# Last self-attention: V stationary in the weighing, a fixed place behind q's and k's halves, the division on POOL, and VectorE's output addition ahead of statistics, scaling and quantising

## The reference, cut to what matters

```python
def _L1_attn_ref(x, W_qkv, W_out):
    ...
    q = rotary_embedding(q, seq_len, HEAD_DIM)
    k = rotary_embedding(k, seq_len, HEAD_DIM)
    scale = 1.0 / jnp.sqrt(jnp.asarray(HEAD_DIM, dtype=x.dtype))
    scores = jnp.einsum('bqhd,bkhd->bhqk', q, k) * scale
    mask = jnp.tril(jnp.ones((seq_len, seq_len), dtype=bool))[None, None, :, :]
    scores = jnp.where(mask, scores, NEG_INF)
    weights = jax.nn.softmax(scores, axis=-1)
    out = jnp.einsum('bhqk,bkhd->bqhd', weights, v)
    out = out.reshape(batch, seq_len, NUM_HEADS * HEAD_DIM)
    return jnp.einsum('bsf,fe->bse', out, W_out)
...
x = x + _L1_attn_ref(_layernorm(x, axis=-1), L1_attn_W_qkv, L1_attn_W_out)
x = x + _L1_ffn_ref(_layernorm(x, axis=-1), L1_ffn_weight)
```

## Time and profile before

| | before |
|---|---|
| median of 3 runs | 2555.43 us (2554.0 to 2556.09) |
| the profiled execution: its time | 2553.02 us |
| its span, first to last instruction | 2551.1 us |
| busy: PE, DVE, ACT, POOL | 93%, 71%, 49%, 33% of the span |
| mean granted TensorE clock | 0.969 |

### The profile page before, as it was taken

The page is one execution under the profiler, slowest core; times in us unless marked ns, Lnnn a source line. Parts: engine busy times, 40 slices in busy tenths (PEclk is TensorE's granted clock), DMA queues, the critical chain, the costliest instruction groups (busy, mean ns, idle before and its releaser), DMA issues. The chain is left out here.

```text
span 2551.1 us, 103353 instructions
## 1 busy us (share of the span) xinstructions
PE 2381.0 (93%) x44640; PEld 1961.5 (77%) x44640; DVE 1817.8 (71%) x3828; ACT 1251.6 (49%) x2826; POOL 840.3 (33%) x741
## 2 busy tenths in 40 slices
PE   7999999999989939999996999999997999999997
PEld 6888888888855537888875777777776888888885
DVE  6778777778867872222226888888896788888886
ACT  5666666665545532333225777776763323233232
POOL 3233333333321213344335444444222232323231
PEclk9999999999989959999998999999998999999998
DMA  6455555554414271111116887887772000000000
GB/s 202 139 155 156 153 156 157 157 151 131 112 31 136 79 305 53 50 49 47 51 54 203 240 231 224 227 233 223 214 205 74 3 3 3 11 11 11 11 11 26
DMA packets 199682, 298.98 MB, mean 117 GB/s; under 512 B 29496, under 2 KB 107452, under 8 KB 197952
## 3 DMA queue, kind: packets, MB, share of 16 engines
q1 hardware_dynamic: 192416, 275.58, 36.6%
q0 software_dynamic: 6816, 16.79, 2.0%
HBM read 170.75 MB, written 78.77 MB: 98 GB/s over the span
## 5 line engine op out<-in xcount | busy, mean ns | idle before, releaser
L846 ACT ACTIVATE prob_x<-ps_score_x,neg_max_x 128x257 f32<-128x257 f32 x1024 | 402.6, 479 | 204.8 <-DVE neg_max_x L914 204.8
L914 DVE TENSOR_REDUCE neg_max_x<-ps_score_x 128x2 f32<-128x514 f32 x512 | 328.9, 684 | 103.4 <-PE ps_score_x L730 102.2
L741 PEld LDWEIGHTS ps_v_x<-v_wide_x,probT_x 128*32 128x32 f32 x18432 | 289.3, 109 | 125.4 <-issue 118.4
L741 PE MATMUL ps_v_x<-v_wide_x,probT_x 128*32 128x68 f32 x18432 | 337.0, 224 | 24.8 <-issue 17.9
L938 DVE STREAM_TRANSPOSE probT_x<-prob_x 128x1152 f32<-128x1152 f32 x256 | 344.1, 1344 | 0.1
L1080 POOL TENSOR_TENSOR ctxT_x_lo<-ready,ctxT_x_hi 128x514 fp32r<-128x514 f32 x128 | 153.0, 1195 | 368.7 <-ACT ctxT_x_hi L825 311.8
L2444 POOL TENSOR_TENSOR rot_s<-turned_s,swapped_s 128x512 f32<-128x512 f32 x128 | 164.3, 1295 | 326.9 <-DVE swapped_s L2373 283.9
L1080 POOL TENSOR_TENSOR split<-loaded,split 128x514 fp32r<-128x514 f32 x128 | 153.5, 1200 | 329.4 <-ACT split L825 314.8
L231 PE MATMUL ps_x<-split,w_q_x_hi 128*128 128x258 f32 x1024 | 208.8, 301 | 13.3 <-POOL split L1080 10.1
L1984 DVE TENSOR_TENSOR hid_moe<-ps_up_moe,silu_moe 128x512 f32<-128x512 f32 x71 | 49.1, 692 | 203.5 <-PE ps_up_moe L231 203.5
L730 PE MATMUL ps_score_x<-kT_x,q_x 32*64 32x257 f32 x4096 | 177.6, 402 | 12.6 <-ACT prob_x L846 9.1
(11 more groups left out here) (299 smaller groups left out, 5967.5 us busy)
## 6 DMA issues: line engine op xcount, KB each, us to landing
v_wide_x<-v_x SPq DMA_DIRECT2D x512, 76.5 KB, 2.2
v_out_x<-v_x SPq DMA_DIRECT2D x128, 306.0 KB, 4.0
v_wide_x<-v_out_x SPq DMA_DIRECT2D x512, 76.5 KB, 3.1
ready<-ctx SPq DMA_DIRECT2D x128, 257.0 KB, 3.6
loaded<-ctx SPq DMA_DIRECT2D x128, 257.0 KB, 4.1
gate_whole<-moe_experts SPq DMA_DIRECT2D x32, 256.0 KB, 3.9
lo_out<-gate_whole SPq DMA_DIRECT2D x32, 256.0 KB
w_moe<-lo_out SPq DMA_DIRECT2D x8, 1024.0 KB, 8.7
```

The source lines that it names most:

```text
L741: ins = pe.do.matmul(self.ps_v[r * T:(r + 1) * T, b % 2, :, :], self.probT[b % 3][:, r, n * T:(n + 1) * T], self.v_wide[b % 4][:, :, r, n, ...
L846: act.do.activation(self.prob[b % 3][:, r, 0:S], self.ps[:, r, 0:S], ACT.Exp, bias=self.neg_max[b % 2][:, r:r + 1]).then_inc(*s.exp.at(tag ...
L914: dve.do.tensor_reduce(self.neg_max[b % 2][:, r], self.ps[:, r, 0:S], AX_X, ALU.max, negate=True).then_inc(*s.neg_max.at(tag, b, half))
```

## The change

`weigh` swaps its operands: V is stationary (32 rows, 64 columns), the turned probabilities move (32 columns). The result for heads 2n and 2n+1 stands in partitions 0 to 63 and 64 to 127, with the head pair and the rows of the batch element along the columns, which is the turned layout that the output's projection needs. So `turn_out`, its ring banks and the buffer `attn` go, and ScalarE and VectorE take the high and low part from PSUM at once. Since the sums of the softmax are along another axis there, the probabilities are divided before they are turned: POOL multiplies them by the inverse sums (`even`). The sums come out of the exponential, which is now 16 instructions, one a head, with the maximum as bias column, so the shift and the summing go from VectorE. The weighed V is no longer in banks of its own: four banks `halves` hold the scores in the first half of two, and the output of one batch element in the second half of each.

The order changes too. Scores of g-1 are first in TensorE's step; weighing, now of group g-2, follows q's and k's four halves; then V's first half, q's turns, the output's projection. VectorE begins with mask and maximum, has the four rotations without the low parts between them, then reciprocal, low parts, the addition to X, the next input's split, and only then transposes the probabilities; statistics of the last layer go ahead of the layer norm's.

```diff
@@ class SelfSoftmax
+    def mask(self, dve, g):
+        s, t, e = self.s, self.t, g % 2
+        dve.wait_ge(s.s_score, "s1", g)
...
     def exponent(self, act, g):
-        act.wait_ge(s.s_shift, tag, g)
-        act.do.activation(self.t["prob"][e][:, :], self.t["shifted"][e][:, :], ACT.Exp,
...
+        act.wait_ge(s.s_max, "s1", g)
...
+        for n in range(H):
+            own = slice(n * T, (n + 1) * T)
+            ins = act.do.activation(t["prob"][e][:, own], t["shifted"][e][:, own], ACT.Exp, bias=t["neg_max"][e][:, n:n + 1],
+                                    accum_out=t["sums"][e][:, n:n + 1])
+        ins.then_inc(*s.s_exp.at("s1", g))
+
+    def divide(self, dve, g):
+        s, t, e = self.s, self.t, g % 2
+        dve.wait_ge(s.s_exp, "s1", g)
+        dve.do.reciprocal(t["inv"][e][:, :], t["sums"][e][:, :]).then_inc(*s.s_inv.at("s1", g))
+
+    def even(self, pool, g):
+        s, t, e = self.s, self.t, g % 2
+        by_head = lambda a: a.rearrange("p (h q) -> p h q", q=T)
+        pool.wait_ge(s.s_inv, "s1", g)
+        pool.do.tensor_tensor(by_head(t["prob"][e][:, :]), by_head(t["prob"][e][:, :]),
+                              t["inv"][e][:, :].unsqueeze(2).to_broadcast([P, H, T]), ALU.mult).then_inc(*s.s_even.at(g))
+
+    def turn(self, dve, g):
+        s, t, e = self.s, self.t, g % 2
+        dve.wait_ge(s.s_even, g)
...
     def weigh(self, pe, g, out, v, dv):
...
+        for n in range(H // 2):
+            for x in range(2):
+                h = 2 * n + x
+                c0 = self.order.column[h]
+                for b in range(BPG):
+                    rows = slice(b * T, (b + 1) * T)
+                    ins = pe.do.matmul(out[x * dv:(x + 1) * dv, b, n, :], v[rows, h * dv:(h + 1) * dv], probT[rows, c0:c0 + T],
+                                       start=True, stop=True)
@@ class SelfAttention1, tensor: the new order of a step
+            if before:
+                pe.wait_ge(s.r_qkT, g - 1, 1, self.NB - 1)
+                if g >= 3:
+                    pe.wait_ge(s.a_lo, g - 3, 0)
+                self.soft.scores(pe, g - 1, q_k)
...
             if out:
-                turn_out(g - 2, 1)
+                pe.wait_ge(s.s_v, tag, g - 2, self.NB - 1)
+                if before:
+                    pe.wait_ge(s.s_masked, g - 1)
+                self.soft.weigh(pe, g - 2, self.out, self.v[g % 2], D1)
             if now:
+                project(g, 2, 0)
                 turn(g, 0, 0)
                 turn(g, 0, 1)
```

More of the change, by code:

```diff
@@ L1212, in weigh @@
[L1212 to L1220 removed]
+        ins.then_inc(*s.s_score.at("s1", g))
```

167 lines of the change are left out of this document (59 added, 108 removed).

## The result

The changed kernel takes 2528.87 us (median of 4 runs, 2528.14 to 2536.52) beside 2555.76 for the kernel before on the same chip: a ratio of 0.990, 95% interval 0.9882 to 0.9919. It is 26.9 us faster. The direction and the range hold; the size is off by 10 us, and several terms are off by nearly as much, with both signs, and partly cancel.

The account below looks back on a forecast made before the run. TensorE was taken to bound the last stage, busy for all 17.70 us of an ordinary step. The sum -49.6 + 14.7 - 2.0 = -36.9 us gave 2516.1 us profiled, 2518.5 as median, range 2503 to 2562.

Parts of the forecast that it names:

- The gain on TensorE: Last stage: eight output transposes gone (0.88 us) and weighing 0.67 shorter; step 17.70 to 16.15 us, 49.6 over 32 steps.
- the weighing: TensorE's 128 records with 32 moving columns on eight tiles: 1.25 us instead of 1.92, bounds 0.9 and 1.92.
- The changes of tile form: Between TensorE's products of different tile shapes: as many as before, their cost only moves, so nothing added.
- the estimate of 1.80 us: Weighing by the skill's overhead rule, 60/64 of 1.92 us: halving columns buys almost nothing, sum 17.6 us worse.
- VectorE's lateness behind the quantising: Next mask 2.7 us late, so the next output's projection waits 2.1 us; seven such steps lose 14.7 us.
- That step is 17.0 long on TensorE: Step with the next input's transposes and quantising: 17.0 us on TensorE, next mask starting at 4.0 instead of 1.33.
- The 0.28 us of the old waits: Waiting in each input-transpose step of the kernel before, 2.0 us in all, contained in the new loss and so subtracted.
- ScalarE: Sixteen exponentials with sums at 250 ns each, 4.0 us together, hidden up to 0.34 us each; cost put at zero.
- The rival: Exponentials become the bound at 458 ns each, some 2566 us; slower from about 0.42 us each; chance 0.15.
- POOL: Division as one 128x512 product, priced like the rotation's 1.29 us, ending at about 14.0 in the step; costs nothing.
- Start and end: Both ends of the stage: no output turning, but exponentials, division and transpose in a row; zero, within 3 us either way.
- the rival of the clock: Clock falls in waits of 2 us before the projection, at most 17 us more: 2535 us; chance 0.10.

Follow-up runs that it names:

- the faster variant: Changed kernel with the next input's transposes, and ScalarE's and VectorE's copies of them, moved ahead of the output's projection: 2517.86 us, ratio 0.9854 to the kernel before.

## Why the prediction was right or wrong

**The gain on TensorE** was forecast as 1.55 us a step and is 1.27, in the early steps 1.38. Right: the eight transposes, 0.88, in full. Mis-sized: the weighing, 1.42 instead of 1.25, inside its bounds. And "The changes of tile form between products are as many as before, so what they cost only moves" is right in the count and wrong in the cost: in front of a small product half of it had been hidden, 0.1 us. Over 30 steps the two are 8 us.

**The reason for the weighing's gain was half wrong.** The prediction said that the products "stream 32 columns where they streamed 64, and lie on eight tiles where they lay on four", and read a row as saying that "fewer columns pay". They hardly do: 64 columns on eight tiles take 1.50 us, 32 on four 1.87, where 32 on eight take 1.42 and 64 on four took 1.92. Tiles are worth 0.42 to 0.45 us, columns 0.05 to 0.08. The sentence of the Trainium skill that was weighed there (TensorEngine Tiling (Array Packing), Performance Considerations, Instruction Overhead), that few columns cost as much as 60, agrees with these runs; the estimate of 1.80 us worked out from it failed because it left out what eight tiles hide. Taking the score product's row as the nearest saved the number, since it had eight tiles too. That number, 1.25 for 1.42, is partly luck: its reason was the columns. Scores take 9.5 ns a record and the weighing 11, a difference that stays open.

**VectorE's lateness behind the quantising**: the right wait in the right step, 0.77 us and 0.23 of slower restart instead of 2.1. The working had TensorE's step at 17.0; it was 18.0, 0.3 since ordinary steps are longer and 0.7 since TensorE itself waited for a bank there, so the mask came 1.9 late and not 2.7. And of what an ordinary step loses on VectorE, the 0.48 us for the high part is made up when it is late (0.05 there), which the working left out; the 0.27 for POOL's rotation is not (0.26 there). Six such steps lie between the first scores and the last but one; they lose 6 us instead of 14.7 for seven.

**The step that failed** in the sum is "That step is 17.0 long on TensorE": it has no term for the ring of banks, which wasn't counted through for the new order. Putting the last layer's transposes ahead of V's second half gave it the bank of the input's first transpose. It costs 0.7 to 1.0 us in five steps, 4 us; the faster variant takes it away, with the wait behind it. The 0.28 us of the old waits did go, as forecast.

**ScalarE**: 0.305 us each instead of 0.25, hidden as forecast in an ordinary step; behind a quantising they have no cover left. Six more exponentials put the limit at 0.36, where the forecast had 0.34. The rival needed 0.42 to be slower than before; it had 0.305. **POOL**: the division takes 1.05 us, and nothing waits for it but VectorE's transpose, 2.3 us in all. That its sums and products stand in the way of VectorE's scalings could not be seen in the changed kernel, where scaling and quantising lie outside them; it decides as soon as they are moved.

**Start and end** were put at zero within 3 us either way, and this failed too. The scores are first in the step now: the first of them come 6.6 us earlier, but from the last but one to the end it takes 61.9 us where it took 51.0, so both ends cost 4.3. The forecast also had two steps' gain in them, 3.1 us, so it is off by 7.4 here, more than by the bank. At the end the sixteen exponentials, reciprocal, division and transpose stand one behind the other and the weighing comes a step later; the wait before the output's projection is 5.73 us, where the longest of the earlier trace rows is 2.98:

```profile
2484.20 1.97 PE L1222 MATMUL ps_halves_s<-probT_s,loaded 32*64 32x32 f32 x128 [1.94 <-DVE shifted_s L1175]
2491.90 0.55 PE L231 MATMUL ps_s<-w_out_s_hi,attnT_s_hi 128*128 128x256 f32 x1 [5.73 <-DVE attnT_s_lo L2380]
```

**The sum again**, for the two profiled executions, over the 30 steps from the first scores to the last but one: the first step -0.5, six early ones -8.5, 23 of the others at -1.27 = -29.2; the bank +4.0; behind the quantising +6.0 (six times 1.0, the first one's odd length in it); the old waits 5 x -0.28 = -1.4; holes in TensorE's stream, mostly inside the scores, +0.6, since both profiles have three. Together -29.0, and so measured. With the 4.3 for both ends that is the span's -24.6, but for rounding.

Against the forecast's -36.9 that is 12.3 short: 8.3 on TensorE's gain in 30 steps, 7.4 at the ends, 4.0 for the bank, 0.6 each for the holes and for old waits counted too often, and 8.7 back, because the lateness was priced too high. These are 12.3 us but for rounding. That the forecast missed by 12 us and not by 21 is luck: this last error ran against the others.

The granted clock fell behind one of the holes, to 0.61 from 2276.30 to 2280.00, and behind none of the waits in these 30 steps; the rival of the clock did not come.

## What to carry to other kernels

When a step's order changes, count the ring of buffers through again for the new order: who takes whose bank, and how old is that bank. Here one bank cost 4 us. Moving the input's transposes ahead of the output's projection took that wait and VectorE's lateness away together and gave 8 us back; at 2516 to 2518 us that is the fastest version here.

The ends of a pipeline have a price of their own: a chain made longer by an operation or a step is hidden in the middle and paid in full at the end.

For many small products, count the tiles that are in turn before the columns: with four, the time until a tile is free again set the pace here; with eight it was nearly hidden. And count the instructions: hundreds of them at 10 ns each can outrun their supply.

Idle time on VectorE is not free for every operation. Ask what POOL does in it.

## What the runs showed of the hardware that I had not expected

- A scaling of 128x256 from SBUF to SBUF on VectorE takes 0.35 to 0.41 us alone and 1.1 to 1.45 when POOL is at a sum or product of 128x512, but 0.41 beside POOL's power of 128x4. A reduction (L1195, 0.69 us) and operations with an operand in PSUM kept their times to 0.05 us beside POOL's sums.
- Small products on one tile are 56 to 60 ns apart for 32 and 64 moving columns alike, behind a first round of 79 to 106; from tile to tile 7 ns.
- TensorE's stream behind a wait of 0.4 to 1.0 us costs another 0.23 to 0.28 us until it runs full again, at a granted clock of 1.00.
- 256 small records in a row, at 9 ns each, are broken by 1.9 to 2.6 us in which TensorE issues nothing, each time until just behind the landing of a 16 KB packet of instructions. 128 in a row are broken so only now and then.
